# Graph sums of a GNN: fp32 selection products, and bf16 products of rows split into three parts

## The chip, the cores and the metric

One Trainium2 chip, one core of it. The metric is the time of one execution on the device in microseconds (us), the median of several runs.

## The reference, cut to what matters

Two layers of graph network with feed-forward parts between them, over 12,500 nodes and 212,500 edges sorted by destination. The change touches the two graph sums of the first layer:

```python
def gcn_conv(x, src, dst, ew, W, b):
    deg = segment_sum(ew, dst); dis = where(deg > 0, rsqrt(deg), 0)
    norm = dis[src] * ew * dis[dst]
    h = x @ W
    return segment_sum(norm[:, None] * h[src], dst) + b
h = relu(gcn_conv(x, src, dst, ew, W1, b1))   # 256 -> 64
z = relu(gcn_conv(h, src, dst, ew, W2, b2))   # 64 -> 32
x_hat = sigmoid(relu(z @ Wd1 + bd1) @ Wd2 + bd2)
```

Self loops are added to the edges. After it come a mixture of four experts, an attention over the same edges with eight heads, and a feed-forward part for the half of the rows with the highest weights.

## The kernel before, in words

The program is a row of stages on five engines which speak through semaphores; each stage ends in a barrier of all engines. The edges stand in 1760 *steps* of 128; a step belongs to one window of 128 destination nodes. Four steps are a *quad* (440 in all), eight a *section* (220). The 100 windows are treated in 25 *groups* of four windows, some 17.6 quads each. Which window a step adds to is data: seven bits for each step in a word per quad (`wpack`), which VectorE loads into a register and unpacks (`quad_windows`, L763).

**The gather (L733).** GpSimd issues one indirect DMA a step (L743), which fetches 128 rows of a table in HBM, one per edge. It runs ahead: 64 gathers may be on their way (the wait for `arrived`), and `rows` has 128 slots, freed by TensorE's products (the wait for `mm_done`, L738). SP collects their arrivals in order and counts quads (L748).

**First sum (`first_sum`, L789), rows of 64 numbers.** ScalarE builds for each step a 128 x 128 selection matrix in fp32: |column - place| by eight activations (L831), then one Relu of 1 - x over the section (L835). It stores them to HBM (`seld`, L838), where the node stage and the attention read them again. VectorE weighs the rows of the next quad by the edge weights (L913). TensorE multiplies the selection, as the fp32 weights of the array, with the rows (L977), one product for each step, into a ring of four PSUM tiles. VectorE adds each product to the accumulator's window (L926); each add waits for the one before it, since both may hit the same window. After each group VectorE scales the sums and adds a bias (L936, L937), TensorE transposes and multiplies with the next weights, and VectorE scales the result into the second table and `acc2` (L945, L947). In passing, early in the stage, VectorE computes flags for the attention (L900 to L904).

**Node stage (`nodes`, L1004), rows of 32.** SP reads the selections of a quad from HBM three quads ahead (L1092). VectorE weighs (L1395), TensorE multiplies (L1146), VectorE adds (L1409), into two PSUM banks in turn. Between the quads, at places written out by hand in `segment`, each engine does its part of the previous group: latent, decoder, sigmoid, normalisation, gates, experts and the attention's projection. On VectorE these are among others the addition of the sigmoid (L1500), the gates (L1439 to L1468), the gated experts (L1476), the second addition (L1512), statistics (L1419, L1423) and copies of transposes (L1435).

**Attention** gathers rows of 272 numbers with the same 1760 steps (L1652), weighs (L1975), multiplies in fp32 (L1865) and adds (L2006). It is not touched by the change, and it goes on reading the fp32 selections.

The add of the first sum, with what leads to it:

```python
ws = quad_windows(dve, K, q)
if q + 1 < QUADS:
    weigh(q + 1)
dve.wait_ge(mm_done, s + QUAD)
for k in range(QUAD):
    to = K.acc1[:, ds(ws[k], 1), :].rearrange("p a c -> p (a c)")
    dve.wait_ge(added, s + k + 1)
    tt(to, to, pm[i % RING][:, k, :], ALU.add).then_inc(added, 1)
```

## Time and profile before

| | us |
|---|---|
| median of three runs | 7882.07 |
| lowest, highest | 7879.19, 7885.58 |
| span of the profiled execution | 9552.9 |
| TensorE matmul busy | 5037.1 |
| VectorE busy | 3724.9 |
| ScalarE busy | 2471.4 |
| GpSimd busy | 5342.4 |

The span is that of one execution with the hardware profiler on, from its first to its last instruction; of that execution no other time is given. It is 1671 us longer than the median without the profiler. PE is TensorE, DVE VectorE, ACT ScalarE, POOL GpSimd. A row of a group has, after the bar, its busy time in us, the mean of one in ns, and after the next bar the engine's idle time just before these instructions, by what ended it: an instruction of another engine, "issue" (nothing that the profile shows) or "remote" (a semaphore whose origin is not found). An fp32 matmul leaves two records, a bf16 one leaves one. [...]

### The profile page before, as it was taken

Reading aid. Unit: us, or ns where it says so; the run is one execution under the profiler, and the core shown is the slowest. Engines: PE = TensorE matmul, PEld = TensorE weight load, DVE = VectorE, ACT = ScalarE, POOL = GpSimd, SP = SyncE. Lnnn points to the kernel's source line nnn. Section 1 sums busy time; section 2 is a strip of 40 time slices with the busy share of each in tenths; the row PEclk is TensorE's granted clock in tenths of the full one; section 3 lists DMA queues with packets and bytes.
Section 4 is the critical chain, followed back from the end, with each engine's and each line's share of the span. In section 5 each row is a group of like instructions: output and inputs, shape, how many; then the busy total and the mean of one; then the engine's idle time right before and its main releaser. Section 6 shows DMA issues by size and latency. Waiting matters only on the chain. (4 is left out here: it accounts for less than half of the span.)

```text
span 9552.9 us, 92056 instructions
## 1 busy us (share of the span) xinstructions
PE 5037.1 (53%) x20272; PEld 3734.0 (39%) x20272; DVE 3724.9 (39%) x10912; ACT 2471.4 (26%) x5104; POOL 5342.4 (56%) x5456
## 2 busy tenths in 40 slices
PE   5323333333333556665565656465566666666469
PEld 4323333333333444444444445243334333443236
DVE  7222222222222222222222223476667666766601
ACT  4323333323332111111111112233333333333111
POOL 0466666666664655555555553466666666666241
PEclk7555555555555566666666666667666666666679
DMA  4222222222222222222222222355555555555220
GB/s 138 61 54 70 69 69 67 72 66 72 65 70 59 63 62 63 65 63 62 62 65 61 63 64 67 105 166 159 163 166 175 158 161 169 171 164 161 83 72 19
DMA packets 577232, 903.66 MB, mean 95 GB/s; under 512 B 170816, under 2 KB 302888, under 8 KB 576038
## 3 DMA queue, kind: packets, MB, share of 16 engines
q0 software_dynamic: 205072, 353.98, 15.4%
q1 hardware_dynamic: 218582, 334.15, 11.3%
q10 hardware_dynamic: 153040, 209.63, 6.4%
q8 instruction: 181, 2.97, 0.1%
q14 instruction: 357, 2.92, 0.1%
HBM read 712.32 MB, written 210.89 MB: 97 GB/s over the span
## 5 line engine op out<-in xcount | busy, mean ns | idle before, releaser
L1652 POOL DMA_INDIRECT att_rows<-ft_rows,edges x1760 | 1841.3, 1046 | 1197.5 <-issue 506.8
L743 POOL DMA_INDIRECT nod_rows<-table,sources x1760 | 1668.1, 948 | 1318.8 <-issue 1206.1
L743 POOL DMA_INDIRECT conv_rows<-table,sources x1760 | 1675.2, 952 | 947.2 <-issue 507.2
L1865 PE MATMUL att_pm<-att_rows,att_sel 128*128 128x264 f32 x3520 | 1458.6, 563 | 486.0 <-issue 345.5
L977 PE MATMUL conv_pm<-conv_rows,conv_hot 128*128 128x64 f32 x3520 | 851.1, 424 | 1560.1 <-DVE conv_rows L913 873.4
L977 PEld LDWEIGHTS conv_pm<-conv_rows,conv_hot 128*128 128x128 f32 x3520 | 782.7, 328 | 1628.8 <-issue 1559.1
L1865 PEld LDWEIGHTS att_pm<-att_rows,att_sel 128*128 128x128 f32 x3520 | 874.8, 271 | 851.4 <-issue 476.9
L926 DVE TENSOR_TENSOR acc<-acc,conv_pm 128x64 f32 x1760 | 388.1, 221 | 1828.0 <-remote 1122.9
L1146 PE MATMUL nod_pm<-nod_rows,nod_sel 128*128 128x32 f32 x3520 | 665.0, 345 | 730.2 <-DVE nod_rows L1395 471.1
L1146 PEld LDWEIGHTS nod_pm<-nod_rows,nod_sel 128*128 128x128 f32 x3520 | 651.2, 272 | 808.5 <-DVE nod_rows L1395 488.2
L1409 DVE TENSOR_TENSOR acc<-acc,nod_pm 128x32 f32 x1760 | 330.7, 188 | 1520.0 <-remote 708.4
L831 ACT ACTIVATE conv_hot<-iota,edges 128x128 f32<-128x128 f32 x1760 | 537.5, 388 | 1422.9 <-remote 1083.4
L2006 DVE TENSOR_TENSOR sums<-sums,att_pm 128x264 f32 x1760 | 747.6, 425 | 317.4 <-issue 161.6
L1975 DVE TENSOR_TENSOR att_rows<-att_rows,moments 128x1056 f32<-128x1056 f32 x440 | 549.5, 1249 | 17.6 <-issue 10.3
L913 DVE TENSOR_TENSOR conv_rows<-conv_rows,edge_w 128x256 f32<-128x256 f32 x440 | 189.0, 429 | 186.0 <-issue 166.4
L835 ACT ACTIVATE conv_hot<-conv_hot,ones 128x1024 f32<-128x1024 f32 x220 | 252.5, 1148 | 7.1
L1741 ACT ACTIVATE a<-att_pxr 1x128 f32<-1x128 f32 x220 | 65.3, 391 | 723.3 <-PE att_pxr L1839 463.8
L2367 PE MATMUL ffn_py<-ffn_w2t,ffn_h 128*128 128x256 f32 x784 | 187.8, 395 | 81.1 <-issue 53.6
L1164 PE MATMUL nod_big<-nod_dw,nod_dt 128*128 128x256 f32 x200 | 93.6, 649 | 246.4 <-ACT nod_dt L1321 239.6
L1731 ACT ACTIVATE att_sel_t<-att_sel_t,ones 128x2048 bf16<-128x2048 bf16 x110 | 220.2, 2002 | 3.6
L1726 ACT ACTIVATE att_sel_t<-att_bc,ncol 128x2048 bf16<-128x2048 bf16 x110 | 218.4, 1985 | 5.5 <-DMA att_bc<-places 5.5
L2324 POOL DMA_INDIRECT out<-ffn_bs,picked x49 | 47.0, 960 | 297.3 <-DVEq L2395 286.3
(387 smaller groups left out, 6536.3 us busy)
## 6 DMA issues: line engine op xcount, KB each, us to landing
selections<-conv_hot ACTq DMA_DIRECT2D x220, 512.0 KB
nod_sel<-selections SPq DMA_DIRECT2D x440, 256.0 KB
att_sel<-selections SPq DMA_DIRECT2D x440, 256.0 KB
att_bc<-places SPq DMA_DIRECT2D x110, 512.0 KB
conv_rows<-table,sources POOLq DMA_INDIRECT x1760
nod_rows<-table,sources POOLq DMA_INDIRECT x1760
att_rows<-ft_rows,edges POOLq DMA_INDIRECT x1760
ft_rows<-nod_ft ACTq DMA_DIRECT2D x25, 544.0 KB
```

Of the source, the lines that this page charges most:

```text
L743: pool.indirect_dma_start(out=rows[:, k % SLOTS, :], out_offset=None, in_=table, in_offset=bass.IndirectOffsetOnAxis(ap=K.srct[:, k:k + 1] ...
L831: ins = act.activation(hot[:, part, k, :], K.iota[:, :], ACT.Abs, bias=K.edges[:, 1, s:s + 1], scale=-1.0)
L835: act.activation(hot[:, part, :, :], hot[:, part, :, :], ACT.Relu, bias=K.ones[:, 0:1], scale=-1.0).then_inc(made, 1)
L926: tt(to, to, pm[i % RING][:, k, :], ALU.add).then_inc(added, 1)
L977: ins = nc.tensor.matmul(pm[i % RING][:, k, :], hot[:, q * QUAD // SECT % PARTS, (q * QUAD + k) % SECT, :], rows[:, (q * QUAD + k) % SLOTS ...
L1146: ins = mm(pm[bank][:, k, :], sel[:, slot * QUAD + k, :], rows[:, ((q + i) * QUAD + k) % SLOTS, :], start=True, stop=True)
L1409: tt(to, to, pm[(at_ + i) % 2][:, k, :], ALU.add).then_inc(added, 1)
L1652: pool.indirect_dma_start(out=rows[:, k % SLOTS, :], out_offset=None, in_=K.ftd, in_offset=bass.IndirectOffsetOnAxis(ap=sources[:, k:k + 1 ...
L1731: act.activation(sel_t[:, :, :], sel_t[:, :, :], ACT.Relu, bias=K.ones[:, 0:1], scale=-1.0).then_inc(t_ready, 1)
L1865: mm(pm[(b * SEGS + s) % LEAD][:, 0:WIDTH], sel[:, s, :], rows[:, slot(i, s), 0:WIDTH], start=True, stop=True).then_inc(mm_done, 1)
L1975: tt(r, r, p.unsqueeze(3).to_broadcast([P, QUAD, HEADS, H1]), ALU.mult).then_inc(weighed, 1)
L2006: tt(at[k], at[k], pm[(order[k] - LEAD) % LEAD][:, 0:WIDTH], ALU.add).then_inc(added, 1)
```

## The change

In both sums the weighed rows are split into three bf16 parts (high, middle, low) that stand side by side; selections are bf16; one bf16 matmul per step multiplies the selection with all three parts (192 columns in the first sum, 96 in the node stage), and the sums of the three parts are kept apart in an fp32 accumulator `accp`, three times as wide. When a group is finished, the three are added up with the old accumulator.

Per quad VectorE has five operations (weigh; copy to bf16; subtract; copy to bf16; subtract) in place of one, and wider adds. In the first sum these five stand between the adds and run two quads ahead; in the node stage they stand in a row ahead of the adds, one quad ahead. In both, the registers of all four windows are computed ahead of them (`lower_ap`). The first sum's `rows` has 64 slots in place of 128, and gathers wait for the split (`parted`) in place of the product. ScalarE makes each section twice (fp32 `wide` with one buffer, and bf16 `hot`) and stores both. TensorE waits only for the split; the last of the five waits for the selections. The node stage reads the bf16 selections, four quads ahead with eight slots. `accp` is zeroed: in the first sum half by VectorE and half by ScalarE, in the node stage by VectorE.

```diff
@@ gather_rows
-        if j >= SLOTS:
-            pool.wait_ge(mm_done, j + SECT - SLOTS)
-        if j >= LANES:
+        if j >= slots:
+            pool.wait_ge(parted, (j + SECT - slots) // QUAD)
+        if j >= LANES and slots > LANES:
             pool.wait_ge(arrived, (j + SECT - LANES) // QUAD)
@@ first_sum
-    RING, C, PARTS, AHEAD = 4, CH1, 4, 3
+    RING, C, PARTS, AHEAD = 3, CH1, 4, 3
+    LEAD, SPLITS, SLOTS1 = 2, 4, LANES
-        hot = ph.sb("hot", [P, PARTS, SECT, P])
+        parts = ph.sb("parts", [P, SPLITS, QUAD, 3, C], BF16)
+        accp = ph.sb("accp", [P, W, 3, C])
+        hot = ph.sb("hot", [P, PARTS, SECT, P], BF16)
+        wide = ph.sb("wide", [P, SECT, P])
@@ ScalarE, per section
+                    if section > 0:
+                        act.wait_ge(wide_stored, section * 16)
+                    act.activation(wide[:, :, :], hot[:, part, :, :], ACT.Relu, bias=K.ones[:, 0:1], scale=-1.0
+                                   ).then_inc(widened, 1)
+                    act.wait_ge(widened, section + 1)
                     act.activation(hot[:, part, :, :], hot[:, part, :, :], ACT.Relu, bias=K.ones[:, 0:1], scale=-1.0
                                    ).then_inc(made, 1)
+                    act.dma_start(K.seld[section * 2:section * 2 + 2].rearrange("q p f -> p q f"),
+                                  wide[:, :, :].rearrange("p (q i) n -> p q (i n)", i=QUAD)
+                                  ).then_inc(wide_stored, 16)
@@ VectorE, per quad
+                def weighed():
+                    dve.wait_ge(arrived, q + 1)
+                    tt(r, r, w, ALU.mult).then_inc(split, 1)
+                def high():
+                    dve.wait_ge(split, q * 4 + 1)
+                    dve.tensor_copy(part(0), r).then_inc(split, 1)
+                def left():
+                    dve.wait_ge(split, q * 4 + 2)
+                    tt(r, r, part(0), ALU.subtract).then_inc(split, 1)
...
+                def low():
+                    dve.wait_ge(split, q * 4 + 4)
+                    dve.wait_ge(made, q * QUAD // SECT + 1)
+                    tt(part(2), r, part(1), ALU.subtract).then_inc(parted, 1)
...
+                    to = [accp[:, ds(w, 1), :, :].rearrange("p a c f -> p (a c f)") for w in quad_windows(dve, K, q)]
+                    for a in to:
+                        dve.lower_ap(a)
+                    if ahead:
+                        weighed()
                     dve.wait_ge(mm_done, s + QUAD)
+                    add(0)
+                    if ahead:
+                        high()
+                    add(1)
...
@@ biased_sums
+                own.then(tt(u[:, :, :], K.acc1[:, ds(g * GW, GW), :], of_part(0), ALU.add))
+                own.then(tt(u[:, :, :], u[:, :, :], of_part(1), ALU.add))
+                own.then(tt(u[:, :, :], u[:, :, :], of_part(2), ALU.add))
@@ TensorE, first sum
-                        ins = nc.tensor.matmul(pm[i % RING][:, k, :], hot[:, q * QUAD // SECT % PARTS, (q * QUAD + k) % SECT, :],
-                                               rows[:, (q * QUAD + k) % SLOTS, :], start=True, stop=True)
+                        ins = nc.tensor.matmul(sum_of(q, k), hot[:, q * QUAD // SECT % PARTS, (q * QUAD + k) % SECT, :],
+                                               parts[:, q % SPLITS, k, :, :].rearrange("p c f -> p (c f)"),
+                                               start=True, stop=True)
@@ nodes
-    RING = QUAD
+    RING, LEAD, SPLITS = 8, 1, 2
+            own.did(dve.memset(accp[:, :, :, :], 0.0))
@@ add, nodes
-                    if q + i + 1 < QUADS:
-                        weigh(q + i + 1)
-                    ws = quad_windows(dve, K, q + i)
+                    to = [accp[:, ds(w, 1), :, :].rearrange("p a c f -> p (a c f)")
+                          for w in quad_windows(dve, K, q + i)]
+                    for a in to:
+                        dve.lower_ap(a)
+                    if q + i + LEAD < QUADS:
+                        for part_of in row_parts(q + i + LEAD):
+                            part_of()
                     dve.wait_ge(mm_done, s + QUAD)
```

## Rows read from the trace of the kernel before

**Rows 1.** The page, its first line.

```profile
span 9552.9 us, 92056 instructions
```

**Rows 2.** Windows of the three gather stages, then of 3100 to 5900 us.

```profile
core 0: us, PE busy (x) PEld busy (x) DVE busy (x) ACT busy (x) POOL busy (x), PEclk, DMA share, GB/s
332.00:2892.00 2560.00, 857.02 (x3564) 784.34 (x3564) 563.96 (x2150) 761.03 (x1904) 1675.19 (x1760) 0.50 0.24 67
2982.00:5878.00 2896.00, 1662.59 (x6516) 1256.08 (x6516) 752.52 (x3275) 464.00 (x738) 1667.59 (x1760) 0.65 0.24 63
6027.00:8917.00 2890.00, 1724.74 (x6486) 1105.01 (x6487) 1938.00 (x4282) 915.03 (x1720) 1841.03 (x1760) 0.67 0.55 163
3100.00:5900.00 2800.00, 1667.04 (x6529) 1259.56 (x6529) 750.68 (x3266) 472.30 (x749) 1585.03 (x1672) 0.65 0.25 64
```

**Rows 3.** Groups of instructions, GpSimd's three gathers.

```profile
L1652 POOL DMA_INDIRECT att_rows<-ft_rows,edges x1760 | 1841.3, 1046 | 1197.5 <-issue 506.8 <-PE att_pm L1865 502.9 <-ACT edges L1769 149.1
L743 POOL DMA_INDIRECT conv_rows<-table,sources x1760 | 1675.2, 952 | 947.2 <-issue 507.2 <-remote 340.2 <-POOLq L96 63.5
L743 POOL DMA_INDIRECT nod_rows<-table,sources x1760 | 1668.1, 948 | 1318.8 <-issue 1206.1 <-POOLq L96 90.5 <-SPq L753 22.0
```

**Rows 4.** Timeline of GpSimd, 1557 to 1565 us: start, us, engine, line, idle before.

```profile
1558.52 0.94 POOL L743 DMA_INDIRECT conv_rows<-table,sources  x1 [0.30 <-issue]
1563.12 0.94 POOL L743 DMA_INDIRECT conv_rows<-table,sources  x1 [3.65 <-remote]
```

**Rows 5.** Groups on VectorE, first graph sum.

```profile
L926 DVE TENSOR_TENSOR acc<-acc,conv_pm 128x64 f32 x1760 | 388.1, 221 | 1828.0 <-remote 1122.9 <-issue 389.7 <-DVE acc L926 250.0
L913 DVE TENSOR_TENSOR conv_rows<-conv_rows,edge_w 128x256 f32<-128x256 f32 x440 | 189.0, 429 | 186.0 <-issue 166.4 <-DVE acc L947 7.7 <-DVE conv_u L937 5.4
...
L947 DVE COPY acc<-conv_tb 128x128 f32 x25 | 5.7, 230 | 6.1 <-DVE conv_tb L945 5.1 <-issue 1.0
...
L902 DVE CAST conv_flb<-conv_fl 128x1806 bf16<-128x1806 f32 x1 | 1.1, 1104 | 0.0
```

**Rows 6.** Groups on VectorE, node stage, 3100 to 5900 us.

```profile
L1409 DVE TENSOR_TENSOR acc<-acc,nod_pm 128x32 f32 x1701 | 319.7, 188 | 1418.4 <-remote 632.1 <-issue 435.4 <-DVE acc L1409 236.1
L1395 DVE TENSOR_TENSOR nod_rows<-nod_rows,edge_w 128x128 f32<-128x128 f32 x425 | 123.0, 289 | 11.0 <-DVE nod_st L1423 5.6 <-issue 2.1
...
L1476 DVE TENSOR_TENSOR nod_e2t<-nod_e,nod_px 128x512 f32<-128x512 f32 x46 | 31.5, 688 | 64.6 <-ACT nod_e L1302 36.7 <-issue 27.9
L1500 DVE TENSOR_TENSOR nod_xg<-nod_xg,nod_sg 128x1024 f32<-128x1024 f32 x24 | 29.5, 1231 | 51.5 <-ACT nod_sg L1323 40.6 <-issue 10.9
L1512 DVE TENSOR_TENSOR nod_xg<-nod_xg,nod_big 128x1024 f32<-128x1024 f32 x23 | 28.1, 1221 | 200.1 <-remote 158.5 <-PE nod_big L1223 41.5
...
L1465 DVE CAST nod_gp<-nod_g 128x60 bf16<-128x60 f32 x23 | 4.7, 206 | 0.8
...
L1439 DVE TENSOR_TENSOR nod_gt<-nod_big,nod_gb 128x16 f32<-128x16 f32 x23 | 4.0, 173 | 30.4 <-PE nod_big L1175 24.7 <-issue 5.7
...
L1458 DVE SCALAR_TENSOR_TENSOR nod_gt<-nod_rank,nod_ex 128x16 f32<-128x16 f32 x23 | 4.0, 176 | 119.2 <-ACT nod_ex L1332 104.9 <-issue 14.3
```

**Rows 7.** Timeline, 4469 to 4474 us, VectorE and TensorE.

```profile
4469.85 0.19 DVE L1409 TENSOR_TENSOR acc<-acc,nod_pm 128x32 f32 x1
...
4471.74 1.91 PE L1146 MATMUL nod_pm<-nod_rows,nod_sel 128*128 128x32 f32 x8
...
4471.95 0.19 DVE L1409 TENSOR_TENSOR acc<-acc,nod_pm 128x32 f32 x1 [0.27 <-issue]
...
4472.44 0.19 DVE L1409 TENSOR_TENSOR acc<-acc,nod_pm 128x32 f32 x1 [0.29 <-issue]
```

**Rows 8.** Timeline of TensorE, 9059 us, bf16 matmuls of 98 columns.

```profile
9059.65 2.22 PE L2174 MATMUL top_prow<-top_named,top_in_part 128*128 128x98 bf16 x25 [18.33 <-DVEq L2269]
```

**Rows 9.** Timeline, 3201 to 3205 us, VectorE beside a gather.

```profile
3201.84 1.23 DVE L1500 TENSOR_TENSOR nod_xg<-nod_xg,nod_sg 128x1024 f32<-128x1024 f32 x1
3202.24 1.65 POOL L743 DMA_INDIRECT nod_rows<-table,sources  x1 [0.31 <-issue]
```

More of the change, by code:

```diff
@@ L742, in gather_rows @@
         for k in range(j, j + SECT):
-            pool.indirect_dma_start(out=rows[:, k % SLOTS, :], out_offset=None, in_=table,
+            pool.indirect_dma_start(out=rows[:, k % slots, :], out_offset=None, in_=table,
                                     in_offset=bass.IndirectOffsetOnAxis(ap=K.srct[:, k:k + 1], axis=0)
@@ L947, in table_rows @@
                 own.then(dve.tensor_copy(K.acc2[:, ds(g * GW, GW), :], tb[:, :, :]))
-            PER = 4
+            PER = 7
             dve.sem_inc(added, 1)
             dve.sem_inc(turned, 1)
+            own.then(dve.memset(accp[:, 0:W // 2, :, :], 0.0))
             dve.wait_ge(loaded, 32)
-            weigh(0)
+            for q in range(LEAD):
+                for part_of in row_parts(q):
+                    part_of()
+            dve.wait_ge(cleared, 1)
             sums(0, 0, FIRST[0] // 2)
@@ L1060, in nodes @@
         ft = ph.sb("ft", [P, GW, RW])
-        pm = [ph.ps(f"pm{i}", [P, QUAD, C]) for i in range(2)]
+        pm = [ph.ps(f"pm{i}", [P, QUAD, 3 * C]) for i in range(2)]
         px = ph.ps("px", [P, 2, GW * P])
@@ L1096, in put @@
                 sp.dma_start(t, src_).then_inc(loaded, 16)
-            for q in range(RING - 1):
+            for q in range(RING // 2):
                 selections(q)
@@ L1140, in products @@
                     bank, slot = (at_ + i) % 2, (at_ + i) % RING
[L1141 to L1144 removed]
+                    pe.wait_ge(row_parted, q + i + 1)
                     for k in range(QUAD):
                         ins = mm(pm[bank][:, k, :], sel[:, slot * QUAD + k, :],
[L1147 removed]
+                                 parts_of_rows[:, (q + i) % SPLITS, k, :, :].rearrange("p c f -> p (c f)"),
+                                 start=True, stop=True)
                     ins.then_inc(mm_done, QUAD)
@@ L1413, in scale @@
                 dve.wait_ge(added, q * QUAD + QUAD)
-                tt(u[:, :, :], K.acc2[:, ds(g * GW, GW), :],
+                of_part = lambda c: accp[:, ds(g * GW, GW), c, :]
+                own.then(tt(u[:, :, :], K.acc2[:, ds(g * GW, GW), :], of_part(0), ALU.add))
+                own.then(tt(u[:, :, :], u[:, :, :], of_part(1), ALU.add))
+                own.then(tt(u[:, :, :], u[:, :, :], of_part(2), ALU.add))
+                tt(u[:, :, :], u[:, :, :],
                    K.dis[:, ds(g * GW, GW)].unsqueeze(2).to_broadcast([P, GW, CH2]), ALU.mult).then_inc(scaled, 1)
```

120 lines of the change are left out of this document (76 added, 44 removed).

## The prediction

> **What bounds the kernel now.** I read first the span [rows 1], then the windows of the three stages that gather rows [rows 2], then GpSimd's groups and its timeline. The span is 9552.9 us, the median of the timed runs 7882.07 us: the profiled execution is 1671 us longer, so it can't be summed as it stands. GpSimd issues 1760 gathers in each of three stages. In the timeline one follows the other after 0.30 us, and takes 0.94 us; now and then there is a pause of several us [rows 4]. Busy mean plus 0.305 us, times 1760 [rows 3], gives 2212 us for the first sum (952 + 305 ns), 2205 for the node stage (948 + 305) and 2378 for attention (1046 + 305): 6795 us. The windows hold 2560, 2896 and 2890 us [rows 2], 1551 us more. That is nearly all of the 1671 us which the timed runs do not have. I conclude that the pauses belong to the profiled execution, where much idle time is put down to "remote", and that the timed kernel runs its three stages at the pace of GpSimd's issue. The rest of the span, 1207 us, plus 6795 is 8002, 1.5% above the median; I sum differences to 7882.
>
> So a group of 17.6 quads (440 in 25 groups) is paced at 17.6 x 4 x 1.253 = 88.2 us in the node stage and 88.5 in the first sum. VectorE and TensorE cost time only where they need more than that, or where they lengthen a gather.
>
> **The change, part by part.** *TensorE.* Eight fp32 records (four matmuls) take 1.91 us, about 0.213 each, 1.71 per quad; bf16 matmuls of 98 columns follow each other at 2.22 / 25 = 0.09 us or less [rows 7, 8]. A quad falls to some 0.35 us in the node stage and 0.7 with 192 columns: 600 us and 440 us of TensorE work disappear in all. Beside a gather pace of 5.0 us per quad this work is already covered, so by itself it gains 0; what it could gain in waits is a rival.
>
> *VectorE, first sum.* A quad has three two-input operations of 256 elements at 429 ns, two casts and four adds of 192 columns. The cast is not there at this size: from 230 ns (copy of 128 elements) and 1104 ns (cast of 1806) [rows 5] I take 0.27 us, bounds 0.23 and 0.43. The add goes from 188 ns at 32 columns to 221 at 64 [rows 5, 6], 1.03 ns a column, so 353 ns at 192. Sum 1.29 + 0.54 + 1.41 = 3.24 us. The interleaving hides the waits for VectorE's own results; about 0.5 us of register work stays: 3.75 us, 66 us a group, 69 with the five operations of the biased sums. Covered by 88.5: 0 us. If that cover went, it would be the whole 440 x 1.4 us.
>
> *ScalarE* has 761 us of work in 220 sections now, 3.5 us each [rows 2]; a second Relu and a second store can't double it, and even 7 us would fit in the 10 us that a section's gathers take. The single wide buffer must be stored within a section; the DMA share of 0.24 [rows 2] leaves room for that. 0 us. The adds are queued behind the wait for rows two quads ahead, but the last quads have no such wait, and gathers may run 64 steps, 80 us, ahead of the splitting: halving the slots costs 0.
>
> *VectorE, node stage.* Here the steps of a quad are not interleaved. Now one quad takes 2.10 us (4469.85 to 4471.95) [rows 7]. The gap between adds is 0.29 us, while an operation that only waits for the one before it follows after 0.8 / 23 = 0.035 us (the cast's idle time) [rows 6]. So 0.25 us per add is register work, and the change puts all of it, with the load of the window word, in one block ahead of the splitting. I estimate 1.25 us for it (four times 0.25 plus 0.25 of the load; bounds 0.9 and 1.5). Then three operations of 289 ns, two casts at 0.25 and five hand-overs of 0.035, 1.54 us; then three intervals of 254 + 35 ns, 0.87. That is 3.66 us, 64.4 a group instead of 37.0. VectorE's other work is (750.7 - 319.7 - 123.0) over the 24.15 groups of the window [rows 2, 6], 12.8 us; some 50 hand-overs add 1.8, three more additions 1.0. Together 80.0 us, under 88.2, but VectorE also waits. Before L1476, L1500, L1512, L1439 and L1458 it waits 307 us for named releasers, 12.7 us a group; with what is put down to "remote" at L1512 it is 19.3 [rows 6]. These waits are for ScalarE and for TensorE's other work, which the change leaves. 80.0 + 12.7 = 92.7, which is 4.5 over the pace: **25 x 4.5 = +113 us**. Bounds: 0 (waits under 8.2 us), and +278 with 19.3. Before, 37.0 + 14.6 + 12.7 = 64 us was hidden. Late next: the splitting, hence TensorE's product, hence the group's scale.
>
> *GpSimd's gathers.* A gather that starts while VectorE runs an operation with two inputs in SBUF is longer: the one at 3202.24 takes 1.65 instead of 0.94 us, and L1500 ended 0.83 us after its start [rows 9]. So the loss is what is left of the operation less 0.12 us. With 0.8 starts per us an operation of length d costs 0.8 (d - 0.12)^2 / 2: 0.038 us for 0.429. For 440 of them that gives 17 us; the gathers' mean of 952 against 944 ns says 14 [rows 3]. With the two casts of 0.27 us a quad's five operations cost 3 x 0.038 + 2 x 0.009 = 0.133 us, 59 us in all, times 14/17, less the 14 of now: **+35 us** in the first sum. Bounds: +20 (casts harmless), and +238 if each of the 880 casts stops GpSimd for its full 0.27 us; I take the low value because the stage's 25 copies of 230 ns [rows 5] don't show in the gathers' mean. In the node stage such a loss falls below VectorE's pace and isn't added. [...]
>
> *Clearing.* 19,200 elements are zeroed ahead of the node stage's VectorE work, 12 to 20 us at 0.61 ns an element (the cast of 1806) or 1.04 (289, 429 and 1231 ns for 128, 256 and 1024) [rows 5, 6]; VectorE is then the pace, so **+15 us**. In the first sum half of it is ScalarE's and the gathers' lead covers it.
>
> Sum: 7882 + 35 + 113 + 15 = **8045 us**.
>
> **Rivals.** (a) *All of VectorE's new work stays hidden*, since its waits shrink with TensorE's: 7882 + 35 + 15 for gathers in the node stage = 7932. For it: many waits are for TensorE, which gets a quad done 1.4 us sooner. (b) *VectorE's waits stay at 19.3 us*: 7882 + 35 + 278 + 15 = 8210. Against: "remote" waits looked like the profile's own. (c) *Casts stop GpSimd for their whole length*. VectorE's casts and GpSimd's gathers meet at 880 places per stage: 238 in the first sum, 8.8 us a group in the node stage, 7882 + 238 + 220 + 15 = 8355. Against: 25 copies of 230 ns [rows 5] left the gathers' mean at 952, 8 ns over the usual 944. (d) *Faster: TensorE paces the node stage now.* [...] Place: the products between ScalarE's steps; it decides if a group takes over 88 us in the timed runs. If 6 us a group, 150 us, are such an excess and the bf16 products end it, 7882 - 150 + 35 + 15 = 7782. Against: floors and rest already reach 8002. (e) *Nothing measurable*: gathers lose as little as now, VectorE is covered: 7882.
>
> **Numbers.** Chances: forecast 0.43, (a) 0.22, (b) 0.12, (c) 0.05, (d) 0.08, (e) 0.10. A measurement of this kernel can tell 0.2%, 16 us. Slower by more than that: 0.43 + 0.22 + 0.12 + 0.05 = 0.82; within 0.10; faster 0.08. The range 7905 to 8290 holds the forecast with its bounds, (a) and (b), and leaves out (c), (d) and (e), 0.23; the forecast's own upper bound is 8210.
>
> **What the profile after would show.** The span may well be shorter although the time is longer: half of the products' records on TensorE are gone and with them pauses. VectorE's adds should be near 353 and 254 ns, its casts 0.23 to 0.3 us, a node quad without waits near 3.7 us and a first-sum quad under 4. The gathers' mean should rise from 952 to some 975 ns in the first sum and stay under 965 in the node stage. GpSimd should show waits for the splitting semaphore in the node stage and none in the first sum; VectorE should be busy over 80% of a node stage in the timed sense. I am wrong if node quads take below 3.2 us, or if gathers keep 944 ns beside casts, or if the timed result lies under 7866.

## The result, and the profile after

The median goes from 7881.28 us (7879.19 to 7885.58, the kernel before, run beside it) to **7931.61 us** (7922.15 to 7933.02). The ratio is 1.0061, interval 1.0049 to 1.0073: slower by 0.6%, some 50 us. The forecast was 8045; the sign and the range held, the size was three times too large.

The page's first line of the kernel after, which answers to [rows 1]:

```profile
span 7930.8 us, 86910 instructions
```

This profile has none of the pauses of [rows 1] and is as long as a timed run. So the two first profiles can't be subtracted from each other, and a run of the kernel before was made again among the experiments (`before_again`); its profile has no pauses either. Both in a row, by the windows of the three gather stages (they answer to [rows 2]), the kernel before first:

```profile
core 0: us, PE busy (x) PEld busy (x) DVE busy (x) ACT busy (x) POOL busy (x), PEclk, DMA share, GB/s
332.00:2546.00 2214.00, 922.14 (x3808) 839.35 (x3808) 580.36 (x2304) 801.83 (x2004) 1668.02 (x1760) 0.50 0.29 80
2562.00:4780.00 2218.00, 1692.53 (x6764) 1276.42 (x6764) 794.01 (x3382) 483.81 (x770) 1671.21 (x1754) 0.70 0.32 83
4866.00:7350.00 2484.00, 1647.78 (x6505) 1092.41 (x6506) 1929.63 (x4287) 917.36 (x1721) 1821.39 (x1752) 0.71 0.63 189
```

The kernel after:

```profile
core 0: us, PE busy (x) PEld busy (x) DVE busy (x) ACT busy (x) POOL busy (x), PEclk, DMA share, GB/s
332.00:2546.00 2214.00, 426.50 (x2044) 249.44 (x2044) 1282.73 (x4118) 1062.27 (x2225) 1677.26 (x1760) 0.50 0.37 106
2566.00:4781.00 2215.00, 1216.72 (x4876) 760.58 (x4877) 1368.73 (x5127) 472.15 (x750) 1678.29 (x1760) 0.68 0.24 58
4908.00:7391.00 2483.00, 1632.33 (x6488) 1078.34 (x6489) 1929.86 (x4281) 919.31 (x1720) 1824.56 (x1760) 0.72 0.64 190
```

PEclk is TensorE's granted clock as a share of its full speed, the mean over the window; the trace holds stretches of 0.5 and of 1 alone. TensorE loses 496 and 476 us, VectorE gains 702 and 575 us, and the length of the gather stages doesn't move. What is longer lies between them. A ledger of both profiles, from the starts and ends of gathers in the timeline of GpSimd:

| stretch, us | before | after | change |
|---|---|---|---|
| start to the first gather | 334.6 | 332.4 | -2.2 |
| first to last gather, first sum | 2204.1 | 2213.4 | +9.3 |
| to the first gather of the node stage | 16.1 | 20.4 | +4.3 |
| first to last gather, node stage | 2213.0 | 2214.4 | +1.4 |
| **to the first gather of attention** | 87.5 | 127.4 | **+39.9** |
| first to last gather, attention | 2488.4 | 2482.6 | -5.8 |
| to the end | 538.7 | 540.1 | +1.4 |

The timeline of the kernel before (`before_again`) at the end of the node stage (start, us, engine, line, idle before) has the last gather, the last add and attention's first gather:

```profile
4766.84 0.94 POOL L743 DMA_INDIRECT nod_rows<-table,sources  x1 [0.30 <-issue]
...
4781.24 0.19 DVE L1409 TENSOR_TENSOR acc<-acc,nod_pm 128x32 f32 x1 [0.29 <-DVE acc L1409]
...
4855.27 1.08 POOL L1652 DMA_INDIRECT att_rows<-ft_rows,edges  x1 [87.48 <-ACT edges L1769]
```

The same in the kernel after:

```profile
4779.70 0.94 POOL L743 DMA_INDIRECT nod_rows<-table,sources  x1 [0.30 <-issue]
...
4831.27 1.12 DVE L1502 TENSOR_TENSOR nod_accp<-nod_accp,nod_pm 128x96 f32 x4 [4.57 <-PE nod_pm L1212]
...
4908.04 1.08 POOL L1750 DMA_INDIRECT att_rows<-ft_rows,edges  x1 [127.40 <-ACT edges L1867]
```

The last add ends 13.6 us behind the last gather before, 51.7 us after. The other 74 to 76 us are the rest of the last groups' work, in both. So VectorE ends the stage 38 us later against the gathers than it did. How it gets there: I paired each add with the gather of its step. The shortest lag in each stretch of 70 steps (about a group) is 8.7 to 8.8 us all through the stage before, and 11.9 in the ten steps left over at its end. After, it is 9, 9, 9, 12, 14, 16, 18 us in the first seven stretches, 38, 40, 42, 44 in the last four and 51 in the ten steps at the end. **VectorE falls behind the gathers by some 1.6 us per group** (35 us over 22 groups). Nothing shows on GpSimd until the stage ends: in this stage a gather may run some 64 steps, 80 us, ahead of the arrivals that SP has counted, and SP counts up to four quads, 20 us, ahead of TensorE's products.

The size of this lag differs between single executions. Five profiles among those below have the node stage of the change as it is (one with another clearing), and their stretch to attention's first gather is 114.7, 116.1, 127.4, 127.5 and 131.1 us; the six that have another order of it or the old form have 83.8 to 87.5.

VectorE's groups, 2700 to 4700 us, after (they answer to [rows 6]):

```profile
L1502 DVE TENSOR_TENSOR nod_accp<-nod_accp,nod_pm 128x96 f32 x1556 | 392.1, 252 | 76.6 <-PE nod_pm L1212 36.0 <-issue 0.2
L1484 DVE TENSOR_TENSOR nod_parts_of_rows<-nod_rows,nod_parts_of_rows 128x128 bf16<-128x128 f32 x389 | 115.5, 297 | 13.7 <-DVE nod_parts_of_rows L1479 0.4
L1475 DVE TENSOR_TENSOR nod_rows<-nod_rows,nod_parts_of_rows 128x128 f32<-128x128 f32 x389 | 114.7, 295 | 13.4
L1467 DVE TENSOR_TENSOR nod_rows<-nod_rows,edge_w 128x128 f32<-128x128 f32 x388 | 113.3, 292 | 340.5 <-issue 256.1 <-SPq L753 83.8
L1471 DVE CAST nod_parts_of_rows<-nod_rows 128x128 bf16<-128x128 f32 x389 | 99.5, 256 | 13.6
L1479 DVE CAST nod_parts_of_rows<-nod_rows 128x128 bf16<-128x128 f32 x389 | 94.3, 242 | 13.3
...
L1610 DVE TENSOR_TENSOR nod_xg<-nod_xg,nod_big 128x1024 f32<-128x1024 f32 x22 | 26.9, 1222 | 55.6 <-PE nod_big L1290 55.6
...
L1555 DVE SCALAR_TENSOR_TENSOR nod_gt<-nod_rank,nod_ex 128x16 f32<-128x16 f32 x23 | 4.0, 175 | 130.7 <-ACT nod_ex L1399 130.7
```

A quad in this stage, in the timeline of VectorE, after (it answers to [rows 7]):

```profile
4793.72 1.11 DVE L1502 TENSOR_TENSOR nod_accp<-nod_accp,nod_pm 128x96 f32 x4
4795.73 0.29 DVE L1467 TENSOR_TENSOR nod_rows<-nod_rows,edge_w 128x128 f32<-128x128 f32 x1 [0.90 <-issue]
4796.06 0.23 DVE L1471 CAST nod_parts_of_rows<-nod_rows 128x128 bf16<-128x128 f32 x1
4796.32 0.29 DVE L1475 TENSOR_TENSOR nod_rows<-nod_rows,nod_parts_of_rows 128x128 f32<-128x128 f32 x1
4796.65 0.23 DVE L1479 CAST nod_parts_of_rows<-nod_rows 128x128 bf16<-128x128 f32 x1
4796.91 0.29 DVE L1484 TENSOR_TENSOR nod_parts_of_rows<-nod_rows,nod_parts_of_rows 128x128 bf16<-128x128 f32 x1
4797.12 1.11 DVE L1502 TENSOR_TENSOR nod_accp<-nod_accp,nod_pm 128x96 f32 x4
```

From add to add it is 3.40 us: 1.11 for the adds, 0.90 for the register block, 1.39 for the splitting. This is a quad in which nothing is held up. The 223 quads of the stage with no other work of VectorE between them have 3.38 us at least and a median of 3.44. Records of VectorE overlap a little: L1484 from 4796.91 has 0.29 us, and the next adds begin at 4797.12.

### The profile page after: what moved, and what is told of

Read it like the earlier page. It is cut to its first block and busy times, and to the rows that moved or that the text cites. A ratio compares the mean times of both kernels' runs of the same rounds, so it can differ in the third digit from the quotient of the medians.

```text
span 7930.8 us, 86910 instructions
## 1 busy us (share of the span) xinstructions
PE 3964.6 (50%) x16752; PEld 2584.8 (33%) x16752; DVE 5019.4 (63%) x14584; ACT 2735.4 (34%) x5325; POOL 5338.6 (67%) x5456
## 5 line engine op out<-in xcount | busy, mean ns | idle before, releaser
L1043 PE MATMUL conv_pm<-conv_parts,conv_hot 128*128 128x192 bf16 x1760 | 361.9, 361 | 1633.3 <-DVE conv_parts L952 1631.2
L837 ACT ACTIVATE conv_hot<-iota,edges 128x128 bf16<-128x128 f32 x1760 | 537.5, 388 | 721.9 <-PE conv_pm L1043 700.3
L1043 PEld LDWEIGHTS conv_pm<-conv_parts,conv_hot 128*128 128x128 bf16 x1760 | 194.4, 131 | 1791.9 <-DVE conv_parts L952 1750.1
L1212 PE MATMUL nod_pm<-nod_parts_of_rows,nod_sel 128*128 128x96 bf16 x1760 | 186.7, 247 | 935.8 <-DVE nod_parts_of_rows L1484 935.8
L969 DVE TENSOR_TENSOR conv_accp<-conv_accp,conv_pm 128x192 f32 x1760 | 603.4, 343 | 1.7 <-DVE conv_accp L969 0.9
L1502 DVE TENSOR_TENSOR nod_accp<-nod_accp,nod_pm 128x96 f32 x1760 | 443.5, 252 | 88.6 <-PE nod_pm L1212 42.7
L1212 PEld LDWEIGHTS nod_pm<-nod_parts_of_rows,nod_sel 128*128 128x128 bf16 x1760 | 120.8, 115 | 1067.1 <-DVE nod_parts_of_rows L1484 1022.3
L1467 DVE TENSOR_TENSOR nod_rows<-nod_rows,edge_w 128x128 f32<-128x128 f32 x440 | 128.7, 292 | 404.9 <-issue 281.0
L843 ACT ACTIVATE conv_wide<-conv_hot,ones 128x1024 f32<-128x1024 bf16 x220 | 252.5, 1148 | 7.1
L846 ACT ACTIVATE conv_hot<-conv_hot,ones 128x1024 bf16<-128x1024 bf16 x220 | 252.5, 1148 | 7.2
```

Of the source, the lines that this page charges most:

```text
L837: ins = act.activation(hot[:, part, k, :], K.iota[:, :], ACT.Abs, bias=K.edges[:, 1, s:s + 1], scale=-1.0)
L843: act.activation(wide[:, :, :], hot[:, part, :, :], ACT.Relu, bias=K.ones[:, 0:1], scale=-1.0).then_inc(widened, 1)
L846: act.activation(hot[:, part, :, :], hot[:, part, :, :], ACT.Relu, bias=K.ones[:, 0:1], scale=-1.0).then_inc(made, 1)
L969: tt(to[k], to[k], sum_of(q, k), ALU.add).then_inc(added, 1)
L1043: ins = nc.tensor.matmul(sum_of(q, k), hot[:, q * QUAD // SECT % PARTS, (q * QUAD + k) % SECT, :], parts[:, q % SPLITS, k, :, :].rearrange ...
L1212: ins = mm(pm[bank][:, k, :], sel[:, slot * QUAD + k, :], parts_of_rows[:, (q + i) % SPLITS, k, :, :].rearrange("p c f -> p (c f)"), start ...
```

## The experiments

Where a label is told with a ratio, it is against the kernel before on the same chip; the ledger's "tail" is the stretch from the last node gather to attention's first, 87.5 us before and 127.4 after.

**Halves of the change.** `first_only` has the first sum of the change and the node stage of before; `nodes_only` the node stage of the change, the first sum of before, and one line more for ScalarE to make the bf16 selections:

```diff
+                    act.activation(half[:, part, :, :], hot[:, part, :, :], ACT.Copy).then_inc(halved, 1)
+                    act.dma_start(K.selb[section * 2:section * 2 + 2]..., half[:, part, :, :]...)
```

> The first sum as after, the node stage as before. Theory (VectorE falls behind in the node stage, and what it is behind is paid once at that stage's end): the first sum keeps GpSimd's pace, so 7881 plus at most 8 us, 7880 to 7890. Rival (half of the loss comes from the first sum: its doubled stores, its five operations beside the gathers, its clearing): 7900 to 7915.

> The node stage as after, the first sum's VectorE and TensorE work as before; ScalarE also makes and stores a bf16 copy of the selections. Theory (the lag of the node stage): nearly the whole loss, 7920 to 7935. Rival (half from the first sum): 7900 to 7910.

Measured: `first_only` 7895.50 us, ratio 1.0015 (1.0006 to 1.0024), tail 87.4 us; `nodes_only` 7916.41, ratio 1.0040 (1.0027 to 1.0054), tail 114.7, its last add 39.3 us behind the last gather. `first_only` lies between its theory (7880 to 7890) and its rival (7900 to 7915), `nodes_only` 4 us below its theory's range. The two excesses, 0.15% and 0.40%, add up to nearly the 0.61% of the whole. Most of it is the node stage, but the first sum's version is not free.

**The same operations in another order.** `interleaved` keeps all of the change and puts the node stage's five operations between its four adds, as the first sum does:

```diff
-                        for part_of in row_parts(q + i + LEAD):
-                            part_of()
+                        steps[0]()
                     for k in range(QUAD):
                         tt(to[k], to[k], pm[(at_ + i) % 2][:, k, :], ALU.add).then_inc(added, 1)
+                        steps[k + 1]()
```

> As after, but in the node stage the five operations of a quad stand between its four adds, as in the first sum. Theory (VectorE's length per quad sets the lag): without the hand-overs a quad takes about 2.6 us in place of 3.40, 14 us less a group, the lag no longer grows past some 25 us, and the time falls by 35 to 45 us to 7885 to 7897. Rival (the loss is in the gathers, which two-input operations lengthen, or in the rest of the work): no change, 7925 to 7935, with VectorE waiting for rows instead.

Measured: 7892.79 us, ratio 1.0013 (1.0004 to 1.0022), tail 86.3. Its quad in the timeline of VectorE, from weighing to weighing:

```profile
3704.38 0.29 DVE L1467 TENSOR_TENSOR nod_rows<-nod_rows,edge_w 128x128 f32<-128x128 f32 x1 [0.81 <-SPq L753]
3704.59 0.25 DVE L1502 TENSOR_TENSOR nod_accp<-nod_accp,nod_pm 128x96 f32 x1
...
3705.72 0.28 DVE L1484 TENSOR_TENSOR nod_parts_of_rows<-nod_rows,nod_parts_of_rows 128x128 bf16<-128x128 f32 x1
3706.81 0.29 DVE L1467 TENSOR_TENSOR nod_rows<-nod_rows,edge_w 128x128 f32<-128x128 f32 x1 [0.81 <-issue]
```

2.43 us in place of 3.40, with the same nine operations: an add that waits for its forerunner and a splitting step that waits for its own now run in each other's waits. That is 17 us less per group, the lag stays at 8 us, and the stage's whole cost is gone. The lag was the cause of the node stage's part, and it was no more than a matter of order.

**VectorE longer.** `longer` has a memset of 300 elements (308 ns) in each node quad, `longer_900` one of 900 (808 ns):

```diff
                 def weighted():
+                    dve.memset(spare[:, q % 2, :], 0.0)
                     dve.wait_ge(arrived, q + 1)
```

> As after, with one more VectorE operation per quad in the node stage (300 elements of a spare tile are zeroed, 0.2 to 0.29 us of its time, reading nothing). Theory (VectorE paces this stage): 440 times 0.2 to 0.29 us more, all of it in the total: 8020 to 8060, and the lag grows by 5 to 6 us a group until GpSimd must wait. Rival (its work is hidden, and the loss comes from elsewhere): 7925 to 7940.

> The changed kernel with a VectorE memset of 900 elements in place of the 300 ahead of each node quad's weighing (300 took 308 ns; some 0.9 us here). Theory (VectorE is over the pace and nearly each further us counts): 0.6 us a quad more than with 300, 10.4 a group, 260 in the stage; 7986 plus 230 to 265 is 8215 to 8250 us. Rival (VectorE's waits for ScalarE and TensorE, 9.8 us a group with 300, go on giving way, since both engines get ahead of it): half of it, 8100 to 8150.

Measured: 7985.95 us, ratio 1.0131 (1.0115 to 1.0146), last add 95.5 us behind, tail 170.1; and 8172.79, ratio 1.0363 (1.0348 to 1.0377). The direction is the theory's, the size below it both times: 54 us for the 90 to 130 that 8020 to 8060 stood for, and 187 for 230 to 265; 8172.79 lies between the theory's 8215 to 8250 and the rival's 8100 to 8150. VectorE's group period, 2000 us by its number of weighings over 17.6, goes 90.5, 92.6, 99.7 us. The first memset makes the median quad 3.74 us in place of 3.44 (of those with no other work between them), 5.3 us in a group, and the period grows by 2.1. Some 2.3 of the rest came out of the waits for ScalarE and TensorE, which were 12.5 us a group and are 10.2 with it; where the other 0.9 went I did not follow. With 900 elements 8.8 us more go in, the period grows by 7.1, and the waits fall to some 7.9. So **a wait in the middle of a loop is not fixed**: the later VectorE comes, the more of it is taken back. The second step can't be read as VectorE's alone, though: its last add is only 30.2 us behind the last gather, because the gathers themselves went from 954 to 1101 ns (see the memsets at the end).

**TensorE's saving alone.** `one_part` is `first_only` with one bf16 product per step in the node stage, straight from the weighing. It leaves the middle and low parts of the rows out of the second sum.

```diff
-                tt(r, r, K.ew[:, s:s + QUAD]...)
+                tt(thin[:, q % 2, :, :], r, K.ew[:, s:s + QUAD]...)
-                                 rows[:, ((q + i) * QUAD + k) % SLOTS, :], start=True, stop=True)
+                                 thin[:, (q + i) % 2, k, :], start=True, stop=True)
```

> The first sum of the change, and the node stage as before but for its product: the weighing writes one bf16 copy of the rows and one bf16 matmul a step multiplies it with the bf16 selection. It leaves the middle and low parts out of the second sum. VectorE's work is that of before, TensorE's falls by some 1.5 us a quad, 600 us in all. Beside it stands the version with the first sum alone changed, 7895.5 us. Theory (TensorE's time in this stage is covered by the gathers, so its saving is worth 0): 7888 to 7900 us, the last node gather to the first attention gather 85 to 88 us. Rival (the 7.6 us a group that VectorE waits for these products, or TensorE's share of the waits for ScalarE, come out as time): 7870 us or less.

Measured: 7903.83 us beside 7891.68 for the kernel before, ratio 1.0014 (1.0005 to 1.0023); `first_only` had 1.0015. The time itself is 4 us above the range, as the kernel before is 9 us slower there than it was beside `first_only`; the ratios are what can be compared. The tail is 83.8 us in place of 87.4. TensorE's saving in this stage is worth 0, plus or minus what these runs can tell, some 10 us.

**The clearing.** `clear_scalar` clears the node stage's accumulator on ScalarE.

```diff
-            own.did(dve.memset(accp[:, :, :, :], 0.0))
+                act.activation(accp[...], K.iota[:, 0:3 * C]..., ACT.Copy, scale=0.0).then_inc(cleared, 1)
```

> The changed kernel, with the node stage's accumulator cleared by ScalarE in place of VectorE. Theory (VectorE's lag of some 26 us at the stage's start is made good within its first groups, so that the clearing never counts): no change, 7924 to 7938 us. The prediction's term, in which VectorE is the pace from the first quad: 15 us less, 7910 to 7920, and the last add's lag 15 us shorter than 51.7.

Measured: 7936.10 us, ratio 1.0065 (1.0051 to 1.0079) against 1.0061, no change; the last add ends 56.2 us behind the last gather, not 15 us sooner than 51.7. In the groups of VectorE at the stage's start, after, the clearing is one line:

```profile
L1425 DVE MEMSET nod_accp<- 128x9600 f32 x1 | 8.1, 8058 | 5.2 <-issue 5.2
```

It has 9,600 elements and takes 8.1 us. The first lag, 26 us, is the same without it; the rows of the first quads and the set-up behind it come later anyway.

**What the better versions still cost.** `first_only`, `interleaved` and `one_part` all stay 0.13 to 0.15% over before. `nodes_interleaved` is `nodes_only` with the interleaving, `stores_only` is the kernel before with only ScalarE's bf16 copy and store, `before_again` the kernel before.

> The node stage of the change with its five operations between the four adds, the first sum's VectorE and TensorE work as before; ScalarE stores the selections in both types. Theory (VectorE's lag in the node stage makes some 36 us of the 50, and the first sum's new work makes the other 10 by itself): with both undone the time is that of before, 7876 to 7888 us, and the last add ends under 14 us behind the last gather. Rival (the 10 us that the interleaved version still cost come from something that both share: bf16 stores and reads, the accumulator of three parts in the node stage): 7890 us or more.

> The kernel before, once more as a run of its own. It tells how far two measurements of one kernel stand apart (expected ratio 1.000 within 0.1%), and may give a profile of it without the pauses of several us. Theory (pauses of the first profile belong to that execution alone): a span of 7880 to 7895 us, the first sum's stage 2213 to 2217 us from its first to its last gather, the last add 10 to 14 us behind the last node gather. Rival (the profiler always slows this program, by its 5000 records more): 9000 us and above again.

> The kernel before, with ScalarE's second copy of each section in bf16 and its store added; nothing reads them. All else is as before. Four versions that share little but this (the first sum alone changed, the node stage interleaved with either first sum, one bf16 part) all stand 9 to 12 us over before. Theory (the stores, and ScalarE's longer sections with them, cost these 10 us, at the first sum's start and end): 7890 to 7894 us, a ratio of 1.001 or more. Rival (each half of the change has some 10 us of its own, from its accumulator and its longer way to the stage's end): 7880 to 7886 us.

Measured: `nodes_interleaved` 7894.63 us against 7886.62, ratio 1.0012 (1.0003 to 1.0021), tail 85.2; my theory that it would be as fast as before fell. `before_again` 7880.74, ratio 0.9997 (0.9988 to 1.0006), span 7882.4: two measurements of one kernel agree, and the pauses of its first profile belonged to that execution. Its first sum's gathers took 2204 us, 9 less than foretold. `stores_only` 7886.73, ratio 1.0007 (0.9998 to 1.0016): between the two theories, and not told apart from no change. GpSimd's groups show the remainder in small pieces; `before_again`:

```profile
L743 POOL DMA_INDIRECT nod_rows<-table,sources x1760 | 1676.9, 953 | 552.2 <-issue 531.5 <-POOLq L96 16.1 <-PE nod_pm L1146 4.3
L743 POOL DMA_INDIRECT conv_rows<-table,sources x1760 | 1668.0, 948 | 599.5 <-issue 532.1 <-POOLq L96 63.4 <-PE conv_pm L977 4.0
```

after (these lines answer to [rows 3]):

```profile
L743 POOL DMA_INDIRECT nod_rows<-table,sources x1760 | 1678.3, 954 | 556.5 <-issue 529.4 <-POOLq L96 20.4 <-DVE nod_parts_of_rows L1484 5.2
L743 POOL DMA_INDIRECT conv_rows<-table,sources x1760 | 1677.3, 953 | 599.9 <-issue 518.5 <-POOLq L96 63.7 <-DVE conv_parts L952 17.7
```

In `stores_only` the first sum's mean is already 951 ns, although VectorE does there what it did before, and in `nodes_only` and `nodes_interleaved`, whose first sum also has VectorE's old work and the second store, it is 954 and 953 ns with 2215.5 and 2214.2 us from the first to the last gather. The kernel after has 953 ns and 2213.4 us. So **the 9.3 us of the ledger's first sum also appear without any splitting there**; nothing shows them to be due to VectorE's new operations. In that stage of `before_again` 51 of the 440 weighings run while a gather starts, in `stores_only` 97, after 134. In `nodes_interleaved` the node stage has 958 ns. Each such nanosecond is 1.76 us. How the remaining 8 to 12 us divide between these stretches is below what the runs tell for certain.

**When in a gather VectorE's operations fall.** `shifted` puts a memset of 240 elements between the arrival and the weighing in the first sum; `wait_first` adds no operation, and only waits for the rows ahead of the register block:

```diff
+                        dve.wait_ge(arrived, q + LEAD + 1)
                     to = [accp[:, ds(w, 1), :, :]... for w in quad_windows(dve, K, q)]
```

> The changed kernel with a memset of 240 elements (some 0.25 us) on VectorE in the first sum, between the wait for the rows of a quad and their weighing. It tells two things. Room: VectorE needs 3.75 us of a quad's 5.0, with it 4.0, so the lag of its adds behind the gathers stays flat and the stage is no longer; if it is no longer covered, 0.2 us x 440 would show as 50 us or more. Phase: the weighing starts 0.25 us later against the gathers. If losses of gathers come by chance meetings, as the prediction has it, their mean stays at 953 ns within 2 and the time at 7925 to 7940 us. If VectorE's chain is locked to the gathers by their arrival, the shift moves casts and subtractions against the gathers' starts, and the mean moves by 5 ns or more, 9 us or more of time, up or down.

> The changed kernel, where VectorE in the first sum waits for the rows of a quad ahead of the register block and not behind it; no operation is added, the weighing starts some 0.9 us later after the rows' arrival. If gathers are lengthened by chance meetings alone, their mean stays at 953 ns within 2 and the time at 7925 to 7940 us. If VectorE's chain is locked to the gathers by their arrival, its operations with two inputs move against the gathers' starts: the mean moves to 944 to 948, or up to 960 and more, and the time with it by 1760 times that difference, 8 us or more. The quad then takes 3.7 us and more from the arrival on, which the 5.0 still cover: the lag of the adds stays flat.

Measured: `wait_first` 7936.18 us, ratio 1.0068 (1.0055 to 1.0082), against 1.0061 for the change, a difference within their intervals. But the profile has the first sum's gathers at 960 ns in place of 953, and that stage at 2225.2 us, 12 longer; 199 gathers start during a weighing, in place of 134. Seven profiles with this first sum unaltered have means of 953 to 956 ns and 2213 to 2219 us, so 6 to 12 us are the order's. The node stage's tail, 116.1, hides it in the total; it is one of the five above, and those differ by 16 us with next to nothing changed in that stage. Chance would have left the mean where it was. VectorE's quads are started by the arrival of rows, so by the gathers themselves, and a later start moves all of them against the next gather.

The room was there: the shortest lag stays flat at 14 to 15 us in both. `shifted` has 7954.56 us, ratio 1.0084 (1.0070 to 1.0097), mean 966 ns. It is no clean test of the phase, since a gather that starts during the memset takes longer by the rest of both operations (less 0.133 us, median of 77). In the timeline of `shifted`:

```profile
1019.78 0.26 DVE L936 MEMSET conv_spare<- 128x240 f32 x1 [4.45 <-SPq L753]
1019.86 1.26 POOL L743 DMA_INDIRECT conv_rows<-table,sources  x1 [0.30 <-issue]
1019.95 0.36 DVE L937 TENSOR_TENSOR conv_rows<-conv_rows,edge_w 128x256 f32<-128x256 f32 x1
```

The gather loses 0.32 us: the weighing behind the memset ends 0.45 us after the gather's start, and 0.13 less is 0.32.

In the timeline of the kernel after, a quad of the first sum with its gathers, and a weighing at a gather's start:

```profile
1005.02 0.94 POOL L743 DMA_INDIRECT conv_rows<-table,sources  x1 [0.30 <-issue]
...
1005.66 0.41 DVE L939 CAST conv_parts<-conv_rows 128x256 bf16<-128x256 f32 x1
...
1006.26 0.46 DVE L943 TENSOR_TENSOR conv_rows<-conv_rows,conv_parts 128x256 f32<-128x256 f32 x1
1006.27 0.95 POOL L743 DMA_INDIRECT conv_rows<-table,sources  x1 [0.30 <-issue]
...
1006.91 0.42 DVE L947 CAST conv_parts<-conv_rows 128x256 bf16<-128x256 f32 x1
...
1007.50 0.47 DVE L952 TENSOR_TENSOR conv_parts<-conv_rows,conv_parts 128x256 bf16<-128x256 f32 x1
1007.52 0.95 POOL L743 DMA_INDIRECT conv_rows<-table,sources  x1 [0.30 <-issue]
...
1021.20 0.43 DVE L935 TENSOR_TENSOR conv_rows<-conv_rows,edge_w 128x256 f32<-128x256 f32 x1 [3.23 <-SPq L753]
1021.26 1.19 POOL L743 DMA_INDIRECT conv_rows<-table,sources  x1 [0.30 <-issue]
```

At 1021.20 the weighing begins 0.06 us ahead of the gather, which takes 1.19 us in place of 0.94: the 0.37 us that were left of the weighing, less 0.12. At 1007.50 the subtraction begins 0.02 us ahead; the gather keeps its 0.95 us, and the subtraction takes 0.47 in place of 0.42. In that close position, up to 0.04 us ahead, are 277 of the 440 last subtractions (L952) and 227 of the first ones (L943).

What puts them there is in the same lines, and no part of the prediction had it: **the gathers lengthen VectorE's casts**. The cast at 1005.66 takes 0.41 us in place of 0.29 and ends 0.11 us behind the end of the gather at 1005.02; so does the one at 1006.91. Of the 880 casts of this stage 491 are longer than 300 ns, and 478 of these end 115 ns behind a gather's end, within 12 ns. They are those that begin 0.60 to 0.75 us after a gather's start; casts that begin 0.05 to 0.60 us after it take their 286 ns. The subtraction follows 0.18 us behind its cast, which is just where the next gather starts: behind a lengthened cast 478 of 491 subtractions lie within 0.04 us ahead of a gather, behind another one 26 of 389.

## Why the prediction was right or wrong

**The bound, right.** Three stages at GpSimd's pace, the pauses not part of the timed kernel: `before_again` has 2204, 2213 and 2488 us for them against floors of 2212, 2205 and 2378. Only attention's was off, by 110 us that it loses in waits, before and after alike.

**TensorE, right.** 600 us of it gone in the node stage and 440 in the first sum were to gain 0; the windows lose 476 and 496 us of it, and `one_part` gains nothing. Rival (d) falls with that: no run shows its 6 us a group, and with the bf16 products alone `one_part` stays at 1.0014, where `first_only` has 1.0015.

**First sum's VectorE, ScalarE, halved slots: right.** A cast takes 287 ns where no gather meets it (predicted 270) and 349 in the mean, the adds 343 (353). From the weighing to the end of the last subtraction a quad has 2.6 us (1503.86 to 1506.42 in the timeline), with 0.9 for the registers 3.5, predicted 3.75. The shortest lag stays flat at 14 us, so all is covered. The 17.7 us that GpSimd's row puts down to L952 are ordinary gaps of 0.30 us: none in that stage is longer than 1 us. The one thing that I didn't price is the stage's end: 4.3 us more until the next stage.

**The node stage, the step that failed.** "80.0 + 12.7 = 92.7, which is 4.5 over the pace: 25 x 4.5 = +113 us" is a small difference of large numbers; the ledger has 39.9 us for it. The mechanism is the one named, VectorE's chain a little over the gathers' pace, and the late splitting, product and scale show up as lag. Term by term, per group (2000 us hold 389 / 17.6 = 22.1 of them):

| us per group | predicted | measured |
|---|---|---|
| quads, 17.6 x 3.66 | 64.4 | 17.6 x 3.40 = 59.8 |
| VectorE's other work | 12.8 + 1.0 | 14.0 |
| hand-overs, issue; measured, what is left | 1.8 | 4.2 |
| waits for ScalarE, TensorE | 12.7 | 12.5 |
| sum | 92.7 | 90.5 |
| pace of the gathers | 88.2 | 88.6 |
| excess | 4.5 | 1.9 |

The measured waits are those of the window with ScalarE or TensorE as the one waited for, 276 us with the products' 36.0, L1555 with 130.7 the largest; 14.0 is VectorE's 1238.1 us there less the 929.4 of the six lines of a quad. The mis-sized term is the quad, by 0.26 us or 4.6 us a group: I took 1.25 us for the register block and it takes 0.90 (my lower bound), 1.54 for the splitting and it takes 1.39; the adds went the other way, 1.11 for 0.87, as the sum has only three of their four lengths. (3.40 is the quad in which nothing is held up; the median is 3.44.)

The excess of 1.9 us comes from counting whole quads in one window; the lag says 1.6. Times the 22 groups in which it grows that is 35 to 42 us, where the prediction had 113 and the ledger has 39.9. Some of the excess is the gathers' doing. In this stage too a cast that begins late in a gather ends behind it, here by 48 ns (139 of the 147 casts over 245 ns): the two casts take 254 and 242 ns in the mean and 226 undisturbed. That is 19.5 us over the stage, 0.8 us a group. No run takes it away alone, so how much of it comes out as time is not shown.

The waits' 12.7 was read wrongly, and came out near by luck. The prediction calls its 307 us waits "for named releasers", but 59 of them are "issue" in [rows 6]; the named ones are 248, 10.3 us a group. With these its sum would have been 90.3, an excess of 2.1 and +53 us. Its 12.7 also leaves out the products, as the 12.5 does not: without them 10.9 are measured. A third error of the same step is its bounds. 0 and +278 came from the waits alone, though an error of 5% in the quad is already 0.18 x 17.6 x 25 = 80 us. And `longer` shows that the waits give way, by 2.3 of the 5.3 us that it adds to a group, so that such an excess comes out smaller than the sum says.

**Gathers, half right.** +35 us was the term, +9.3 the ledger's. The law on [rows 9], what is left of the operation less 0.12 us, holds for the weighing (0.37 - 0.12 = 0.25, measured 1.19 - 0.94). What failed is "with 0.8 starts per us", an even spread of meetings. Of the three operations with two inputs, two lie mostly where they do no harm: the gathers that start beside L943 and L952 have means of 944 and 945 ns. Of the 9.3 us, 8 come from weighings, now 134 meetings of 1023 ns on average for 51 of 995, and the weighing is the operation that was there before; that the stage is as long in `nodes_only`, without the other four, says the same. A gather starts during a cast 49 times, which costs it 2 us in all: the 20 on L939 and 29 on L947 delay it by 25 and 51 ns, with 136 and 198 ns of them left. Rival (c), the full length of 880 casts, is out. For other operations `before_again` has the node stage: 24 gathers that start during L1500, two inputs in SBUF, take 1442 ns on average; 24 that start during L1512 and 32 during L1476, whose second input is TensorE's sum in PSUM, take 944 and 946 ns, with 686 and 376 ns of the operation left.

**Clearing, wrong.** +15 us was the term, 0 is measured. I had twice the elements (19,200; it is 9,600, 8.1 us), and it lies in a time when VectorE is not yet the pace.

**The rivals.** 7932 of rival (a) is the result to the us by luck, not by its mechanism: VectorE's work is not all hidden, although its waits did shrink, as that rival had it: before, by the same reading of `before_again`, those for ScalarE and TensorE's other work are 13.2 us a group and those for the products 7.9; after, 10.9 and 1.6. Two of its terms, 35 and 15 for gathers and clearing, were wrong by about as much as the lag that it left out. The signs foretold came true in part. The profile is shorter, but not because TensorE's records went: `before_again` has them all and no pauses. The node quad lies between 3.2 and 3.7. The gathers' mean in the first sum is 953, not 975. VectorE is busy 62% of the node stage (1368.7 of 2215 us), not over 80%. GpSimd shows no wait for the splitting in the node stage either: a lag of 51 us fits in its lead, and so do the 95 us of `longer`.

## What to carry to other kernels

Where an engine's chain comes near the pace of the bound one, plot its lag behind it, first event against last: an engine can fall behind all through a stage with no wait to be seen on the bound engine, and be paid for once, at the stage's end. Dependent chains of one engine (adds in a row, a splitting in a row) cost their hand-overs twice here when they stood one behind the other; interleaved they cost 2.43 us for 3.40, which is all the difference in the node stage. And work that is taken from an engine that doesn't bind pays for nothing (496 and 476 us of TensorE's here): neither sum could win by it, and the best form of the change found, `interleaved`, is still 0.13% (0.04 to 0.22%) slower than the kernel before.

## What the runs showed of the hardware that was not expected

- The meetings of VectorE and GpSimd are not chance. The arrival of rows starts VectorE, so the weighing's phase depends on what stands in between: without an operation more on VectorE, `wait_first` went from 134 meetings to 199, and `stores_only` from 51 to 97. The subtractions' phase is set by the casts before them, of which 478 of the 491 lengthened ones end 115 ns behind a gather's end.
- A gather delays a cast too, and not for its whole length: a cast of 256 elements that begins 0.05 to 0.60 us after a gather's start takes 286 ns, one that begins 0.60 to 0.65 us after it 416 ns, and it ends 115 ns behind the gather's end (48 ns for 128 elements).
- The last 0.04 us before a gather's start turn the meeting round. A subtraction (L952, L943) that begins 0.04 us or less ahead of a gather is the one that takes longer (465 ns in place of 419, the mean of 277 on L952 as of 227 on L943, ending 453 to 458 ns behind the gather's start), and the gather keeps 944 ns. A weighing that begins 0.045 us ahead keeps its 426 ns, and the gather takes 1195.
- A memset alone did not lengthen a gather here; with a weighing ready right behind it the gather was longer by the rest of both, less 0.133 us. The memset of 8.06 us at the node stage's start has six gathers starting in it, all of 940 to 945 ns; here are two. The one at the first sum's start is followed by a weighing, but by way of a wait for the memset's own semaphore, and its six gathers take 940 to 947 ns. The 808 ns memset of `longer_900` has the weighing behind it with no wait but that for rows that had long arrived, and its gather takes 1.59 us:

```profile
2567.58 8.06 DVE L1425 MEMSET nod_accp<- 128x9600 f32 x1 [5.16 <-issue]
...
2568.78 0.94 POOL L743 DMA_INDIRECT nod_rows<-table,sources  x1 [0.30 <-issue]
2570.02 0.94 POOL L743 DMA_INDIRECT nod_rows<-table,sources  x1 [0.30 <-issue]
```

```profile
3705.06 0.81 DVE L1467 MEMSET nod_spare<- 128x900 f32 x1 [1.49 <-issue]
3705.23 1.59 POOL L743 DMA_INDIRECT nod_rows<-table,sources  x1 [0.30 <-issue]
3705.78 0.23 DVE L1469 TENSOR_TENSOR nod_rows<-nod_rows,edge_w 128x128 f32<-128x128 f32 x1
```

  In `shifted`, `longer` and `longer_900` alike the median gather that starts during the memset (of 77, 102 and 325) loses the time up to the end of the weighing behind it, less 0.133 us; in `shifted` the 25 that start behind the memset with over 0.14 us of the weighing left lose that rest less the same 0.133 (median). So the mean rose to 1101 ns with 808 ns in each node quad. By what such a gather is held before the weighing begins is not shown.
- One kernel's profile can hold 1671 us of pauses and the next profile of it none.
